# Local attention on one core: the additive mask written into the score banks by ScalarE in place of two mask products on TensorE

## The reference

```
DEPTH, HEADS, DIM_HEAD, WINDOW = 6, 16, 64, 32
q, k, v = split(shift_tokens(x) @ Wqkv)          # 16 heads of 64
q = l2norm(q) * q_scale;  k = l2norm(k) * k_scale
q = q*cos*scale + rotate_half(q)*sin*scale       # k the same with 1/scale
# a window of 32 queries sees the window before it and its own: 64 keys
mask = (it < jb) | (it > jb + WINDOW) | (jb == -1)
sim  = einsum('bhwie,bhwje->bhwij', bq, bk2) * 8.0
sim  = where(mask, -max, sim)
out  = einsum('bhwij,bhwje->bhwie', softmax(sim), bv2)
x    = out @ Wo + x                              # then a gated feed-forward
```

## Time and profile before

| | |
|---|---|
| median of 3 runs | 7207.6 us |
| lowest and highest | 7197.66 and 7215.52 us |
| the profiled execution | 7208.77 us |
| its span, first to last instruction | 7206.7 us |
| mean granted clock of TensorE | 0.823 |
| busy share: TensorE, its weight loads, VectorE, ScalarE, GpSimd | 74%, 47%, 53%, 55%, 33% |

### The profile page before, as it was taken

How to read it: one execution, slowest core, us unless ns; L and a number is a source line. 1 busy time by engine, 2 the same in 40 slices (tenths; PEclk the granted TensorE clock), 3 DMA queues, 4 the chain that set the end, 5 groups by cost and what they waited for, 6 DMA issues and landing times. The chain is left out here.

```text
span 7206.7 us, 178920 instructions
## 1 busy us (share of the span) xinstructions
PE 5312.7 (74%) x69288; PEld 3368.6 (47%) x69288; DVE 3840.9 (53%) x6202; ACT 3985.0 (55%) x8451; POOL 2396.7 (33%) x1351
## 2 busy tenths in 40 slices
PE   1000198888888888977777988888888979687778
PEld 0000065655656564733333655656564747343444
DVE  5555654645455554555554645455554546445854
ACT  4333264646455555539997646555554546355655
POOL 0000162626354444504443626354453535000000
PEclk6555599999999999976666989999998989766876
DMA  1000121212222121200000212212121212000000
GB/s 43 0 0 0 37 51 48 55 49 54 53 49 59 42 53 50 57 11 1 1 1 20 55 47 53 54 45 52 47 57 44 57 45 57 18 2 3 0 2 6
DMA packets 177838, 248.52 MB, mean 34 GB/s; under 512 B 51692, under 2 KB 79848, under 8 KB 175080
## 3 DMA queue, kind: packets, MB, share of 16 engines
q1 hardware_dynamic: 177128, 237.68, 13.2%
HBM read 43.50 MB, written 5.24 MB: 7 GB/s over the span
## 5 line engine op out<-in xcount | busy, mean ns | idle before, releaser
L377 PE MATMUL PS<-arena 128*128 128x512 f32 x2304 | 1163.5, 632 | 220.0 <-ACT arena L500 117.1
L670 POOL TENSOR_TENSOR arena<-arena 128x512 f32<-128x512 f32 x384 | 586.6, 1551 | 651.3 <-DVE arena L622 651.3
L670 POOL TENSOR_TENSOR lns<-arena 128x512 f32<-128x512 f32 x384 | 566.1, 1498 | 666.7 <-DVE arena L622 666.7
L377 PEld LDWEIGHTS PS<-arena 128*128 128x128 f32 x2304 | 412.9, 199 | 646.1 <-issue 359.7
L499 ACT ACTIVATE arena<-PS 128x512 f32<-128x512 f32 x768 | 472.1, 615 | 333.4 <-PE PS L377 258.4
L434 PE MATMUL PS<-arena 64*64 64x32 f32 x24576 | 534.7, 227 | 155.4 <-ACT arena L531 121.4
L592 DVE TENSOR_REDUCE arena<-PS 128x16 f32<-128x1024 f32 x192 | 235.2, 1225 | 731.0 <-PE PS L408 731.0
L1106 PE MATMUL PS<-arena 128*128 128x512 f32 x8 | 6.7, 1019 | 807.8 <-DVE arena L1040 807.8
L434 PEld LDWEIGHTS PS<-arena 64*64 64x64 f32 x24576 | 509.5, 141 | 191.7 <-issue 188.0
L611 DVE TENSOR_REDUCE arena<-arena 128x32 f32<-128x2048 f32 x192 | 438.8, 2285 | 293.4 <-ACT arena L500 286.1
L539 ACT ACTIVATE arena<-PS 128x512 f32<-128x512 f32 x384 | 208.9, 597 | 648.0 <-PE PS L434 648.0
(11 more groups left out here) (254 smaller groups left out, 11101.2 us busy)
## 6 DMA issues: line engine op xcount, KB each, us to landing
arena<-arena SPq DMA_DIRECT2D x2880, 64.0 KB, 2.0
arena<-in_L_ffn_Wqkv SPq DMA_DIRECT2D x12, 1536.0 KB, 6.5
arena<-in_L_ffn_Wo SPq DMA_DIRECT2D x48, 128.0 KB, 6.3
scratch<-arena SPq DMA_DIRECT2D x4, 1024.0 KB, 4.8
arena<-scratch SPq DMA_DIRECT2D x4, 1024.0 KB, 7.6
arena<-in_L_ffn_W SPq DMA_DIRECT2D x12, 341.0 KB
arena<-in_ffn_scales SPq DMA_DIRECT2D x12, 128.0 KB, 5.8
arena<-in_L_ffn_W SPq DMA_DIRECT2D x12, 128.0 KB
```

Of the source, the lines that this page charges most:

```text
L377: pe.matmul(PS[:, QKV + n % 2, :], xs[uu % 2][:, par * P:(par + 1) * P], w, start=True, stop=True).then_inc(qkv_ready, 1)
L670: last = pool.tensor_tensor(heads(t2)[:, :, a:a + 32], heads(raws[par])[:, :, b:b + 32], sine, ALU.mult)
```

## The change

The bf16 copies of identity and mask, and the two products with them, are removed. In their place ScalarE copies the f32 mask, repeated for all 16 heads, into both score banks in one ACTIVATE of 128x1024 (write_mask). It does so in each tile for the next one, right after the exponential, before the copies of the turned q and k. TensorE waits for that copy (mask_ready) in place of scores_read. The score products still add to what the bank holds (start=False). Whether a product adds or overwrites depends on marks that only TensorE sets, so at the entry of each layer TensorE writes both banks once with start=True; ScalarE waits for these two products (banks_marked), writes the first mask, and only then begins to copy the first projection.

```diff
-        ident_b = sb("ident_b", P, BF16)
-        masks_b = sb("masks_b", 2 * 2 * WIN, BF16)
@@ scores, TensorE
-                    wait_alone(pe, scores_read, nth(g, TILES, tt))
-                mask = masks_b[:, par * 2 * WIN:(par + 1) * 2 * WIN].rearrange("p (o j) -> p o j", o=1)
-                pe.matmul(PS[:, SCORE + s, :], ident_b[:], mask.broadcast_to([P, PAIRS, 2 * WIN]),
-                          start=True, stop=False, skip_group_check=True)
+                    wait_alone(pe, mask_ready, nth(g, TILES, tt))
@@ entry of a layer, TensorE, ahead of the first projection
+            for s in range(2):
+
+                pe.matmul(PS[:, SCORE + s, :], ident[:], Wqkv[:, 0:CH], start=True, stop=True).then_inc(banks_marked, 1)
@@ ScalarE
+            def write_mask(g, tt):
+
+                S = PS[:, SCORE:SCORE + 2, :].rearrange("p s (m e) -> p (s m) e", e=FD)
+                act.activation(S, masks[:, tt % 2:tt % 2 + 1, :].broadcast_to([P, FH, 2 * WIN]), ACT.Copy)\
+                   .then_inc(mask_ready, 1)
@@ body, ScalarE
                     exps(g, tt)
                     if ahead:
+                        write_mask(g, tt + 1)
                         copy_turned(g, tt + 1, (0, 1))
@@ entry of a layer, ScalarE
             enter(0, 0)
             enter(1, 1)
+            act.wait_ge(banks_marked, 2 * (run + 1))
+            write_mask(first, 0)
             copy_qkv(first, 0, range(6), False)
@@ GpSimd, once ahead of the six layers
-            pool.tensor_copy(ident_b[:], ident[:]).then_inc(masks_cast, 1)
-            pool.tensor_copy(masks_b[:], masks.rearrange("p t j -> p (t j)")).then_inc(masks_cast, 1)
```

More of the change, by code:

```diff
@@ L224, in program @@
         probs_ready = sem("probs_ready")
-        masks_cast = sem("masks_cast")
+        mask_ready = sem("mask_ready")
+        banks_marked = sem("banks_marked")
         vw_ready = [sem(f"vw_ready{i}") for i in range(2)]
```

## The result

The changed kernel takes 7425.1 us (median of 4 runs, 7404.7 to 7431.1), the kernel before 7211.6 us beside it (4 runs): 1.029 times as long, 95% interval 1.0259 to 1.0321. The change makes the kernel slower, as forecast, but by 214 us in place of 99, and outside the forecast range. The profiled execution has a span of 7429.1 us, 222 us more than that of before.

The account below looks back on a forecast made before the run. The prediction took a loop through ScalarE's copies and VectorE's reduction as the bound: +95.2 us in steady tiles, +10.4 at entries, -6 in last tiles, -1 for casts, +98.6 in all, giving 7307 us, range 7240 to 7367.

Parts of the forecast that it names:

- The bound: Steady tile: projection, ScalarE's copies, VectorE's reduction, norm steps, copy of turned probabilities, heads, second scores, next projection form the loop.
- The write: ScalarE, behind each exponential: 0.94 us, moving the loop by 0.93 us a steady tile; bounds 0.64 and 1.08.
- what the removed products are worth: Steady tiles: the first product worth nothing, ahead of a wait; the second gives back 0.32 us a tile.
- I expect no change: TensorE's granted clock in steady tiles: stays at 1.00, the 2.4 GHz level, despite the longer wait before the heads.
- the tail: Last tiles of a layer: the write fits beside VectorE's work in tile 13; -6 us in all, bounds -15 and +15.
- the hole in the second scores: TensorE's 0.41 us issue hole, taken as unchanged; its two ends were growing by 0.32 us or going.
- A: Rival: the write is hidden in the loop and the kernel gets faster, about 7162 us; chance 0.08.
- B: Rival: TensorE is the bound and both products come back, about 7114 us; chance 0.04.
- C's upper end: Rival: second scores take as long without their product, a tile gets 0.93 us longer, 7357 us; chance 0.15.
- the entries: Start of each layer: marks and first mask delay what follows by 1.5 us, less 0.63 for products; net +10.4 us.
- the last tiles and the rest: End of each layer and outside attention: 0 for the last tiles, -1 us for GpSimd's two removed casts.

Follow-up runs that it names:

- x1: The kernel before with ScalarE's mask write added in each tile and both mask products kept, no marks: 1.0165, 7341 us.
- x4: The changed kernel with three bf16 products of zeros added in TensorE's wait between the first scores and the heads: 1.0137, 7327 us.
- w3: The changed kernel with a bf16 product of zeros at both old places of the mask products: 1.0186, 7351 us.
- w4: The kernel before without the first mask product, bank 0 left without a mask: 1.0065, 7268 us.
- w5: The kernel before without the second mask product, bank 1 left without a mask: 1.0053.
- x2: The kernel before without both mask products and without any mask, scores written with start=True: 1.0026, 7244 us.
- z3: The changed kernel with the mask write moved behind the last copy of the projection, without fillers: 1.0613, 7694 us.
- x3: The changed kernel without the two marking products at a layer's entry and without ScalarE's wait for them: 1.0292, 7436 us.
- z1: The kernel before without mask products in the scores, but with two in TensorE's wait between first scores and heads: 0.9991.
- y4: The kernel before with two more mask products in TensorE's wait before the heads: 0.9937, 7178 us.
- y2: The changed kernel with three zero products in TensorE's wait and the mask write moved behind the projection's last copy: 1.0184.

## Why the prediction was wrong

**The bound: right, with one stretch missing.** L619 waits for L499 in every tile and the heads for L536 in 14 of 16, so the loop runs through ScalarE and VectorE as said. The write is 1.04 us long, 0.96 from start to start (0.94 taken); in x1 it costs the even tiles 0.93 us, as forecast. In the odd tiles it was 20.04 - 19.49 = 0.55 us; of the 0.38 us that are missing, 0.22 are holes in TensorE's issue that the kernel before has there (0.24 us a tile in the mean) and x1 hardly has (0.02). The rest is not accounted for. Over all steady tiles the write is +102 us, where the forecast had 145. The 43 us too many hid part of the error below. TensorE's wait before the heads is 1.16 us a time in the steady tiles, where 1.6 was forecast: ahead of it TensorE waits 0.46 us a time for the turned copies (144 times in the steady tiles), where 0.3 was forecast.

**The failed step: what the removed products are worth.** The prediction put them at 156 x 0.32 = 50 us gained. On top of the write their removal cost 71 us, an error of 121. Two sentences of the prediction carry it.

The first is "The granted clock over 90 us with such waits in every tile is 1.00 ... and I expect no change." The row held for waits of 0.55 to 0.67 us. With 1.1 us and two products fewer, low clock appeared 25 times in the steady tiles. It makes 63 of the 71 us. In the first steady tile it set in 8 times, 1.4 to 1.8 us after a wait of 1.87 us before the heads. Of the 17 times behind that tile, 12 set in 0.7 to 1.3 us after the wait before the heads ended, with no other gap over 0.15 us in the 7 us ahead; the other five came 0.9 to 1.7 us after a hole of 0.93 to 1.26 us put down to "issue".

That the low clock comes from what TensorE does around its waits, and not from ScalarE's write as such, is shown from three sides: by adding work in the wait (x4) or at the old places (w3, x1), by taking products out with no write (w4, w5, x2), and by more waiting (z3). Low clock in us:

| kernel | first steady tile | the other 12 | wait before the heads, us a time |
|---|---|---|---|
| before | 34 | 0 | 0.72 |
| before + write (x1) | 0 | 0 | 0.91 |
| changed + both zero products (w3) | 0 | 3 | 0.90 |
| changed + fillers (x4) | 3 | 12 | 0.47 |
| changed | 55 | 122 | 1.15 |
| changed, no marks (x3) | 85 | 168 | 1.15 |
| before, no products (x2) | 102 | 47 | 0.92 |
| before, first out (w4) | 99 | 34 | 0.90 |
| before, second out (w5) | 106 | 35 | 0.71 |
| changed, write late (z3) | 75 | 1030 | 0.68 |

The mean granted clock of all runs goes with it: 0.810 to 0.818 in x2, w4, w5 and z1, 0.824 to 0.832 in x1, x4, w3 and the kernels before with fillers, 0.762 to 0.777 in z3, and 0.817 to 0.825 in the kernel before beside most of them (0.818 to 0.827 beside y4). The length of the wait before the heads does not say where it falls: x1, w3, x2 and w4 have the same, and in the changed kernel the middle one is 1.10 us both of the 20 tiles with low clock behind the first and of the 124 without. Why it falls in just these tiles is not shown. The forecast of the clock in the tail fails with it: low clock in the two tail tiles went from 52 to 107 us.

The second is "I leave it as it is", of the hole in the second scores. The forecast kept two ends for it, and it went towards the bad one: holes in heads and second scores sum to 71 us in the steady tiles, against 44 before and 39 in x1. Even at full clock the removal gave nothing back: against x1 the even tiles are 0.05 us shorter and the odd ones 0.17 longer, where 0.32 shorter was forecast for both. The even tiles also have ScalarE's copies of new tokens as a second limit, which the prediction did not see; it read the earlier trace rows to the next projection, but not what released that projection. This is the stretch missing in its loop.

**Rivals.** A (write hidden) and B (TensorE the bound) did not come: x2, without products, is slower than before, and B had said 7114 us. C's upper end, 7357 us, is near x1 and w3 (7341 and 7351 us) by luck: they keep both products, so its mechanism is not theirs. The time measured lies above all of them, because no rival had the clock.

**The sum.** In the steady tiles the write came out 43 us below the forecast and the products 121 above it; the entries were 15 below, the tail 35 above, the last tiles and the rest 26 above. That makes the 124 us between 99 and the span's 222. The sign was right for the reason given, the write on the loop.

**The entry.** The working was nearly right and its sum was not. ScalarE and TensorE at the start of the second layer, changed kernel:

```profile
1271.23 1.19 PE L468 MATMUL PS<-arena,ident 128*128 128x512 f32 x1 [5.71 <-issue]
...
1274.40 2.93 PE L468 MATMUL PS<-arena,ident 128*128 128x512 f32 x3 [1.98 <-issue]
...
1277.37 1.04 ACT L529 ACTIVATE PS<-arena 128x1024 f32<-128x1024 f32 x1 [5.35 <-PE PS L468]
1278.53 0.60 ACT L498 ACTIVATE arena<-PS 128x512 f32<-128x512 f32 x1
```

The first copy comes 6.52 us after the tokens are in (1272.01), before 3.80: 2.7 us late, 2.4 forecast. In the mean of the 12 layers it is 1.6 us late. And still the entries are 4.5 us shorter in sum. Low clock in the second cold part of the entry went from 10.2 to 6.8 us in most layers of the first call. The marks do that: x3, without them, has 10.2 us again, and 185 us of low clock in all entries against 136 (182 in the kernel before). But its entries are no longer for it (522.5 us), so the marks cost about what they give back. Kernels with the same entry differ by up to 6.5 us in this sum (526.3 in the changed kernel, 532.8 in x4), so a finer account is not possible. The entry's step that failed is that all that follows moves with the first copy.

**The tail.** Forecast -6 us, measured +29, with x1 at +22: the write is not hidden there. TensorE turns q and k of the next tile ahead of the probabilities, and these turns wait for ScalarE's copies, which stand behind the write. In tile 14 the turned probabilities start 4.6 us behind the exponential in the changed kernel and in x1, 4.0 in the kernel before. In tile 13 of the second layer L417 starts at 1563.25, 5.55 us behind the exponential, before 4.89 us (exponential at 1525.85):

```profile
1557.70 1.06 ACT L524 ACTIVATE arena<-arena 128x1024 f32<-128x1024 f32 x1 [3.28 <-DVE arena L603]
...
1560.42 2.12 DVE L614 TENSOR_TENSOR arena<-arena 128x1024 f32<-128x1024 f32 x1
1560.44 0.30 PE L391 MATMUL PS<-ident,arena 128*128 128x128 f32 x1 [3.39 <-ACT arena L519]
...
1563.25 1.72 PE L417 MATMUL PS<-ident,arena 128*128 128x128 f32 x8
```

VectorE was done at 1562.54; the turns were not, since they began 0.96 us later than before and most of them ran at the low clock. At the full clock the same 16 records took 1.8 us before; by that, an estimate, they would have ended at 1562.2, and the write would have fitted in this tile, as forecast. With the write later (y2) the tail tiles sum to 366.0 us, 3.9 less than before.

**What stays open:** the first steady tile's low clock in the kernels without products; what brings more low clock to the feed-forward (129 us in the ten stretches of the changed kernel, 87 before, 83 in x1, but 138 in w3, whose loop has 3 us); and what sets the holes that the profile calls issue. Their place in the instruction stream is the same in all layers of a call (in the kernel before, the 26th or 44th record of an even tile's second scores in the first call, the 42nd or 60th in the second) and moves when instructions are added or removed.

## What to carry to other kernels

Work in front of a wait was not free to remove here (0.65% slower in w4). Before taking products off TensorE, see from which row its clock would be read afterwards: a row at full clock holds for the waits and the work that it was taken with, not for longer waits with less work. When a change makes TensorE wait longer, compare the sum of its busy time: here fewer instructions with more busy microseconds were low clock. A filler product in the wait is a cheap test, and here a gain of 0.6% on the kernel before.

When an end of the loop is given a saving, look for the second thing that the next instruction waits for. Here the token copies, 4.49 us after the heads, and the holes ate it.

## What the runs showed of the hardware

ScalarE's write of the mask into PSUM is about as long as its exponential into SBUF: 1040 ns against 1067 in the mean for 128x1024 in the changed kernel, 0.96 us from start to start for both. The Trainium skill ("ScalarE: Activation LUTs", "Step-by-step: what each stage is for") calls PSUM the port of lower latency; these rows agree by 27 ns of one instruction, with another function in each, and show no gain from start to start.

A wait of TensorE of about 1 us can be followed by the 1.2 GHz level for the next stages: 12 times in the changed kernel after nothing but such a wait. The prediction named the Trainium skill's "TensorE: Matmul & The Clock Gate", "What's actually happening", for the entry only; that the clock is low unless activity releases it applies inside the loop as well. In kernels with the same loop, low clock in the steady tiles went from 0 to 1105 us by where two bf16 products or one ScalarE write stood, or whether they were there.
